# Transformer block, the pass for the row maxima: four 64x64 tiles instead of full-array matmuls, in eight groups among the first twelve score steps

## What is computed

```
content_score = einsum('bthd,bshd->bhts', q + u_bias, k)
pos_score = einsum('bthd,phd->bhtp', q + v_bias, p)
pos_score = _rel_shift(pos_score)
score = (content_score + pos_score) / math.sqrt(dh)
attn = jax.nn.softmax(score, axis=-1)
ctx = jnp.einsum('bhts,bshd->bthd', attn, v)
```

## Time and profile before

| | us |
|---|---|
| three runs | 1070.51, 1071.98, 1072.19 (median 1071.98) |
| profiled execution, its own time | 1072.0 |
| its span, first to last instruction | 1070.1 |
| busy in the span: PE, PEld | 850.5, 644.0 |
| busy in the span: DVE, ACT, POOL | 723.9, 460.0, 397.1 |
| mean granted clock of TensorE | 0.908 |

### The profile page before, as it was taken

The page is one execution under the profiler, slowest core; times in us unless marked ns, Lnnn a source line. Parts: engine busy times, 40 slices in busy tenths (PEclk is TensorE's granted clock), DMA queues, the critical chain, the costliest instruction groups (busy, mean ns, idle before and its releaser), DMA issues.

```text
span 1070.1 us, 21831 instructions
## 1 busy us (share of the span) xinstructions
PE 850.5 (79%) x8587; PEld 644.0 (60%) x8587; DVE 723.9 (68%) x1573; ACT 460.0 (43%) x773; POOL 397.1 (37%) x446
## 2 busy tenths in 40 slices
PE   2483679999999999987457998999999697057774
PEld 1243468888888888875434655666666377025553
DVE  6772435565555655533577888878788588989994
ACT  3860023333333333334455555656556554222331
POOL 6463001433334334335333334434243207323544
PEclk7696789999999999999669999999999899578998
DMA  6056111333243333453100000000000000000111
GB/s 140 1 159 216 42 39 38 79 75 65 67 94 72 72 65 69 90 153 74 25 1 1 2 2 2 2 2 2 1 2 1 1 1 1 0 0 2 23 26 32
DMA packets 69743, 46.45 MB, mean 43 GB/s; under 512 B 35184, under 2 KB 60984, under 8 KB 68920
## 3 DMA queue, kind: packets, MB, share of 16 engines
q1 hardware_dynamic: 52776, 24.72, 10.2%
q0 software_dynamic: 8032, 19.11, 7.0%
q10 hardware_dynamic: 8832, 1.22, 0.7%
HBM read 30.05 MB, written 12.06 MB: 39 GB/s over the span
## 4 chain that ended last, share of the span: by engine, by line
PE 40%; DVE 27%; DMA 9%; POOL 6%; SPq 6%; ACT 6%; issue 5%; ACTq 0%; POOLq 0%; DVEq 0%
PE PS L1059 7%; PE PS L1174 5%; PE PS L1175 5%; PE PS L1176 5%; PE PS L1079 4%; PE PS L1039 3%; PE PS L1063 3%; PE PS L1040 3%; DMA REG<-inverse_sums 3%; SPq L349 2%; DVE HB L1797 2%; DVE XX L1457 2%; DVE REG L1592 2%; DVE XX L1463 2%; DVE AM L1448 2%
## 5 line engine op out<-in xcount | busy, mean ns | idle before, releaser
L1573 DVE TENSOR_REDUCE MX<-PS 128x2 f32<-128x512 f32 x256 | 171.5, 686 | 165.4 <-PE PS L1040 163.7
L776 ACT ACTIVATE REG<-PS 128x1024 f32<-128x1024 f32 x128 | 131.5, 1027 | 242.1 <-PE PS L1063 239.4
L1059 PE MATMUL PS<-XX,TB 96*128 96x64 f16 x2048 | 160.2, 246 | 7.7 <-DMA XX<-NEG 4.5
L1039 PE MATMUL PS<-TM,YY 128*128 128x256 f16 x512 | 129.6, 285 | 31.7 <-DMA YY<-REG 14.9
L1059 PEld LDWEIGHTS PS<-XX,TB 96*128 96x128 f16 x2048 | 133.6, 120 | 23.2 <-issue 12.8
L613 POOL TENSOR_TENSOR HH<-HB,HH 128x512 f16<-128x512 f32 x64 | 75.8, 1184 | 173.8 <-ACT HH L833 173.8
L1040 PE MATMUL PS<-KM,YY 128*128 128x256 f16 x512 | 126.7, 279 | 0.0
L863 ACT ACTIVATE SG<-PS 128x512 f32<-128x512 f32 x128 | 76.2, 595 | 112.1 <-PE PS L1176 111.8
L1797 DVE SCALAR_TENSOR_TENSOR HB<-PS,SG 128x512 f32<-128x512 f32 x128 | 87.6, 684 | 46.0 <-ACT SG L863 46.0
L1063 PE MATMUL PS<-XX,KC 97*128 97x128 f16 x1024 | 108.0, 229 | 0.0
L1174 PE MATMUL PS<-XH,XX 128*128 128x512 f16 x256 | 98.8, 386 | 10.3 <-DVE HB L1797 10.1
(11 more groups left out here) (235 smaller groups left out, 1653.1 us busy)
## 6 DMA issues: line engine op xcount, KB each, us to landing
REG<-inverse_sums POOLq DMA_DIRECT2D x60, 128.0 KB, 3.1
YY<-queries_content ACTq DMA_DIRECT2D x224, 4.0 KB
KC<-keys_strips SPq DMA_DIRECT2D x16, 192.0 KB
keys_strips<-REG POOLq DMA_DIRECT2D x12, 224.0 KB, 7.8
R<-in_L_attn_x SPq DMA_DIRECT2D x32, 64.0 KB, 2.9
queries_position<-REG POOLq DMA_DIRECT2D x2, 960.0 KB, 12.9
queries_content<-REG POOLq DMA_DIRECT2D x2, 960.0 KB, 16.9
XX<-queries_position SPq DMA_DIRECT2D x60, 32.0 KB
```

Of the source, the lines that this page charges most:

```text
L776: A(P[jt][:, 1024 * up:1024 * up + 1024].rearrange("p (k x) -> p k x", k=2), ST[u % 2], ACT.Exp).then_inc(exp_done, 1)
L1039: mm(o, yp[:, a], TM[p][:, 31 - a:31 - a + T], start=True, stop=False)
L1059: mm(o_pos[:, a], TB[p][0:96, y0:y0 + 128], xp[0:96, 8 * bank + a], start=(a == 0), stop=False, skip_group_check=True)
L1573: nc.vector.tensor_reduce(MX[h % 2][:, 2 * kk:2 * kk + 2], banks[4 + kk % 2].rearrange("p (a j) -> p a j", a=2), AX_X, ALU.max)\
```

## The change

The maxima's matmuls become tiles of 64 rows and 64 columns. YP and YC hold half as many columns, with one half of the batches on partitions 0 to 63 and the other on 64 to 127, and TM's window is there twice. A group g (eight a head) does two offsets i times four tiles: first four position matmuls, then four content matmuls, 256 columns each, into two banks. One reduction takes 128x1024 to 128x4. Head 0's groups use banks 4, 5 and 6, 7 in turn; all later ones use banks 4 and 5 alone and wait for the reduction of the group just before. The groups follow score steps 0, 2, 3, 5, 7, 8, 10, 11, the context parts move to k = 3 and k = 11, and the second half of the shift is waited for at k = 4. Position queries always come from NQB, half by SyncE, half by GpSimd (by ScalarE for head 0); the copy in memory is gone. `shift_row` is four transfers, and XC's columns are laid out so that its content loads are contiguous.

```diff
+BANKS = (0, 4, 2, 6, 1, 5, 3, 7)
 NAT_K, NAT_QV, NAT_QU = 0, 2, 4
+BURSTS = (0, 2, 3, 5, 7, 8, 10, 11)
 
 
...
-    qvb_d = nc.dram_tensor("queries_position_batched", [128, N], F16, kind="Internal").ap()
...
-        YP, YC = ([YY[:, (2 * i + j) * N:(2 * i + j + 1) * N] for j in range(2)] for i in range(2))
+        YP, YC = ([YY[:, (2 * i + j) * N // 2:(2 * i + j + 1) * N // 2] for j in range(2)] for i in range(2))
...
-        Y_LOADS = 16 * (8 + 16 + 2)
...
+        def batch_pair(chunk):
+            b = 8 * (chunk % 2) + chunk // 2
+            return slice(b, b + 5, 4)
+        def maximum_queries(eng, h, src, half, done):
+            for s in range(8):
+                rows = 64 * half + 8 * (7 - s)
+                eng.dma_start(YP[h % 2][rows:rows + 8, :].rearrange("p (n s a) -> p s n a", n=8, s=8)[:, s],
+                              src[:, N // 2 * half:N // 2 * half + N // 2].rearrange("p (n s a) -> p s n a", n=8, s=8)[:, s])\
+                    .then_inc(done[h % 2], 16)
+        def maximum_banks(h, g):
+            return 6 if h == 0 and g % 2 else 4
 
...
-                sp.dma_start(TM[p][0:64, 0:287], window).then_inc(y_in[p], 16)
+                for half in range(2):
+                    sp.dma_start(TM[p][64 * half:64 * half + 64, 0:287], window).then_inc(y_in[p], 16)
 
...
-                                     NAT[NAT_QU + part][rows, :].rearrange("p (c w i) -> p w c i", c=4, w=4)[:, w]).then_inc(x_in[p], 16)
+                        sp.dma_start(XC[p][to:to + 8, 1024 * w:1024 * w + 1024],
+                                     NAT[NAT_QU + part][rows, 1024 * w:1024 * w + 1024]).then_inc(x_in[p], 16)
...
-            gp.dma_start(qvb_d[rest, :], NQB[rest, :]).then_inc(qvb_out, 16)
+            maximum_queries(gp, 1, NQB[DH:2 * DH, :], 1, y_second)
...
+            def later_queries(h):
+                if h < H:
+                    gp.wait_ge(max_mm, 8 * (h - 1))
+                    maximum_queries(gp, h, NQB[DH * h:DH * h + DH, :], 1, y_second)
             def sums_to_dram(h):
 
                 gp.wait_ge(ev_done, h + 1)
                 gp.dma_start(den_d[h % 2].rearrange("(g x) -> g x", g=4), EV[h % 2][DH:128:32, :]).then_inc(den_out, 16)
                 gp.wait_ge(den_out, 16 * (h + 1))
                 gp.dma_start(RC[h % 2][:, :], den_d[h % 2].rearrange("(p x) -> p x", p=128)).then_inc(den_in, 16)
+                later_queries(h + 3)
...
+            later_queries(2)
...
 
                 act.wait_ge(neg_ready, 2 * n + half + 1)
-                row = XC[n % 2][96:97, :].rearrange("p (m t a) -> p t m a", t=2, a=16)
-                act.dma_start(row[:, half], NEG[half][:, :]).then_inc(neg_in[half], 16)
+                row = XC[n % 2][96:97, :].rearrange("p (r m c t a) -> p r c t m a", r=2, m=64, c=2, t=2)
+                for r in range(2):
+                    for c in range(2):
+                        act.dma_start(row[:, r, c, half], NEG[half][64 * c:64 * c + 64, 8 * r:8 * r + 8]).then_inc(neg_in[half], 16)
 
             def content_rows(h, src, batches):
 
...
             act.wait_ge(high_done, 24)
-            for h in range(2):
-                content_rows(h, NAT[NAT_QU][DH * h:DH * h + DH, :], range(B))
+            content_rows(0, NAT[NAT_QU][0:DH, :], range(B))
+            maximum_queries(act, 0, NQB[0:DH, :], 1, y_in)
+            content_rows(1, NAT[NAT_QU][DH:2 * DH, :], range(10))
             shift_row(0, 0)
+            content_rows(1, NAT[NAT_QU][DH:2 * DH, :], range(10, B))
...
-            def maximum_scores(h, kk):
-                p, n = h % 2, 16 * h + kk
-                if kk == 0:
-                    pe.wait_ge(y_in[p], Y_LOADS * (h // 2 + 1))
-                if n >= 2:
-                    pe.wait_ge(max_done, n - 1)
+            def maximum_scores(h, g):
+                p, n, bank = h % 2, 8 * h + g, maximum_banks(h, g)
+                if g == 0:
+                    pe.wait_ge(y_in[p], Y_FIRST[p] + Y_LOADS * (h // 2))
+                    if h:
+                        pe.wait_ge(y_second[p], Y_SECOND * ((h + 1) // 2))
+                if h:
+                    pe.wait_ge(max_done, n)
+                elif g >= 2:
+                    pe.wait_ge(max_done, g - 1)
                 yp = YP[p][:, :].rearrange("p (m a) -> p a m", a=32)
                 yc = YC[p][:, :].rearrange("p (m a) -> p a m", a=32)
-                for half in range(2):
-                    a = 2 * kk + half
-                    o = banks[4 + kk % 2][:, T * half:T * half + T]
-                    mm(o, yp[:, a], TM[p][:, 31 - a:31 - a + T], start=True, stop=False)
-                    last = mm(o, yc[:, a], KM[p][:, :], start=False, stop=True)
+                for i in range(2):
+                    tiles = [(slice(64 * r, 64 * r + 64), 16 * c + 2 * g + i, banks[bank + r][64 * c:64 * c + 64, T * i:T * i + T])
+                             for r in range(2) for c in range(2)]
+                    for rows, a, o in tiles:
+                        mm(o, yp[rows, a], TM[p][rows, 31 - a:31 - a + T], start=True, stop=False)
+                    for rows, a, o in tiles:
+                        last = mm(o, yc[rows, a], KM[p][rows, :], start=False, stop=True)
                 last.then_inc(max_mm, 1)
...
-                    pe.wait_ge(neg_in[0], 16 * (h + 1))
-                elif k == 2:
-                    pe.wait_ge(neg_in[1], 16 * (h + 1))
+                    pe.wait_ge(neg_in[0], 64 * (h + 1))
+                elif k == 4:
+                    pe.wait_ge(neg_in[1], 64 * (h + 1))
...
@@ -1081,25 +1111,24 @@
                 if half:
                     last.then_inc(pv_mm, 1)
 
-            for kk in range(16):
-                maximum_scores(0, kk)
+            for g in range(8):
+                maximum_scores(0, g)
             for h in range(H):
                 for k in range(16):
                     scores(h, k)
-                    if h + 1 < H and k < 12:
-                        for kk in range(16 * k // 12, 16 * (k + 1) // 12):
-                            maximum_scores(h + 1, kk)
-                    if h and k == 4:
+                    if h + 1 < H and k in BURSTS:
+                        maximum_scores(h + 1, BURSTS.index(k))
+                    if h and k == 3:
                         context_part(h - 1, 1, 0)
                         context_part(h - 1, 1, 1)
-                    if k == 12:
+                    if k == 11:
                         context_part(h, 0, 0)
                         context_part(h, 0, 1)
             context_part(H - 1, 1, 0)
             context_part(H - 1, 1, 1)
...
-            def maximum(h, kk):
-                ve.wait_ge(max_mm, 16 * h + kk + 1)
-                nc.vector.tensor_reduce(MX[h % 2][:, 2 * kk:2 * kk + 2],
-                                        banks[4 + kk % 2].rearrange("p (a j) -> p a j", a=2), AX_X, ALU.max)\
+            def maximum(h, g):
+                bank = maximum_banks(h, g)
+                ve.wait_ge(max_mm, 8 * h + g + 1)
+                nc.vector.tensor_reduce(MX[h % 2][:, :].rearrange("p (r a) -> p r a", r=2)[:, :, 2 * g:2 * g + 2],
+                                        PS[:, bank:bank + 2, :].rearrange("p r (i j) -> p r i j", i=2), AX_X, ALU.max)\
                     .then_inc(max_done, 1)
 
             def negate(h, half):
 
-                ve.wait_ge(max_done, 16 * h + 8 * half + 8)
+                ve.wait_ge(max_done, 8 * h + 4 * half + 4)
                 if h:
-                    ve.wait_ge(neg_in[half], 16 * h)
...
+                   MX[h % 2][:, :].rearrange("p (r a) -> p r a", r=2)[:, :, 8 * half:8 * half + 8],
+                   -1.0, None, ALU.mult).then_inc(neg_ready, 1)
 
             def evacuate_context(h):
...
+            for g in range(8):
+                maximum(0, g)
+                if g % 4 == 3:
+                    negate(0, g // 4)
...
+                    for g in range(8):
+                        maximum(h + 1, g)
+                        if g % 4 == 3:
+                            negate(h + 1, g // 4)
+                        if g == 2 and h:
                             evacuate_context(h - 1)
-                        if kk == 14 and h:
+                        if g == 6 and h:
                             inverse_sums(h - 1)
```

More of the change, by code:

```diff
@@ L250, in adaln_program @@
         stored = sem("stored")
+        y_second = [sem(f"y_second{p}") for p in range(2)]
         l_feat, stored_last = sem("l_feat"), sem("stored_last")
@@ L344, in maximum_keys @@
                     .then_inc(y_in[h % 2], 16)
-            def maximum_queries(h, src):
-                for s in range(8):
-                    sp.dma_start(YP[h % 2][8 * (7 - s):8 * (7 - s) + 8, :].rearrange("p (b s a) -> p s b a", b=B, s=8)[:, s],
-                                 src.rearrange("p (b s a) -> p s b a", b=B, s=8)[:, s]).then_inc(y_in[h % 2], 16)
             def first_position_queries(h):
@@ L1117, in _ @@
                 for j in range(4):
```

(19 more changed lines are left out.)

59 lines of the change are left out of this document (29 added, 30 removed).

## The result

| | before | after |
|---|---|---|
| median of 15 runs each, us | 1073.74 | 1084.38 |
| lowest and highest | 1069.55, 1077.78 | 1077.70, 1090.81 |
| ratio of the means, after to before, with 95% interval | | 1.0106 [1.0081, 1.0130] |

The change makes the kernel about 11 us slower, where 1063 and a range up to 1078 were predicted. The profiled execution took 1086.14 us (its span 1084.3). The runs also scatter more than before.

The account below looks back on a forecast made before the run. It took the order of PE's own instructions to bound the heads. Steady heads -4.2, GpSimd +2, before head 1 -3.6, head 2's maxima +1.4 and last head -4.5 sum to -8.9: 1072.0 to 1063 us, range 1051 to 1078.

Parts of the forecast that it names:

- sum of a steady head: Heads 1 to 14: matmuls, new waits and dropped costs together change a head by -0.30 us, -4.2 in all.
- Before head 1: Start of the kernel: without the 896 KB copy SyncE's queue ends sooner, -3.6 us, between -6 and +2.
- last head: Wait for the shift shrinks by about 2 us and most low-clock time goes: -4.5, between 0 and -7.5.
- The exposed load of the first weights: Each maxima group: uncovered loading of its first weights costs 0.05 us, between nothing and 0.11.
- The new wait: Steady heads: a group waits 0.62 us for the previous reduction after one score step, three times a head; none after two.
- ScalarE's six more issues: Steady heads: six more shift transfers at about 0.4 us each cost nothing, at most 0.5 a head.
- GpSimd, +2: Heads: eight new query issues lengthen GpSimd's round by 2.3 us, making early heads' queries late; +2 us in all.
- The sign that was to give GpSimd away: Profile after: a steady period of 22.3 us or more, with no idle before GpSimd's first instruction, speaks for GpSimd.
- Head 2's maxima, +1.4: Head 2's maxima: ScalarE's content rows come behind three more shift transfers, 1.1 us, and 0.3 of head 0's new waits.
- GpSimd as bound: Rival: GpSimd's round, 21.4 to 24.2 us, bounds all heads; total about 1070 us; chance 0.15.
- tiles in turn: Rival: tiles do not run side by side, a round takes 0.22 us instead of 0.11; total 1113 us; chance 0.08.
- dearer switches: Rival: switching the array's shape costs 0.2 us each way, +0.9 a head; total 1076 us; chance 0.09.

Follow-up runs that it names:

- e1: Changed kernel with groups behind steps 1, 3, 4, 6, 8, 10, 11, 13, and the shift's second half behind a head's last exponential: 1077.85 us.
- e5: e1 with four of GpSimd's eight query transfers, for heads 2 on, moved to SyncE: 1058.08 us, ratio 0.9859 to the kernel before.
- e2: Changed kernel with the shift's second half issued in two pairs, behind the exponentials of steps 12 and 13 and of 14 and 15: 1084.09 us.
- e11: Changed kernel in its own order of groups, with four of GpSimd's eight query transfers of heads 2 on given to SyncE: 1087.70 us.
- e9: Changed kernel with head 2's content rows issued behind the first four exponentials of head 0 instead of the last two: 1072.58 us.
- e8: Kernel before the change, with the experts' weights issued only when the last shift has landed: 1069.70 us, ratio 0.9961.
- e12: Kernel before the change, with the experts' weights after the last shift and head 2's content rows behind head 0's first four exponentials: 1059.93 us.
- e6: e5 with the experts' weights issued only when the last shift has landed: 1051.83 us, ratio 0.9816 to the kernel before.
- e3: Changed kernel with the experts' weights issued by SyncE only when the last shift has landed: 1083.79 us, ratio 1.0103 to the kernel before.
- e10: e6 with head 2's content rows issued early as in e9: 1046.64 us, ratio 0.9745 to the kernel before.

## Why the prediction was wrong, by its steps

In short: the step that failed most is the sum of a steady head, where the exposed weight load (0.05 a group) and ScalarE's issues (nothing) were priced too low; the runs show 0.10 and 0.3. The steps on the start ("Before head 1") and on the last head failed next. The form of the steady head, tiles in parallel with three waits, was right.

- **Tiles side by side:** right. **Switches:** in 0.09 and out 0.09 to 0.10, right.
- **"The exposed load of the first weights I put at 0.05 us":** it is 0.10, near the upper bound of 0.11 that was named. A group is 0.75 us (entry 0.09, first round 0.21, two of 0.11, 0.01, exit 0.21, by the start times in the trace), eight are 6.0 instead of 5.52: +0.5 a head. The page TensorE: Matmul & The Clock Gate of the Trainium skill, section LDWEIGHTS (loading the stationary operand), puts a load at columns / 1.2 GHz. An estimate by that page is 53 ns for 64 columns; the trace shows 0.10 behind a switch, with four loads together.
- **The new wait, 0.62 three times a head, none at two steps:** right, 0.63. It was priced rightly and still not seen for what it was: at 1.9 us a head the largest cost of the change, and one of the order alone, as the heads of 20.5 us in e1 and e5 show.
- **ScalarE's six more issues, "nothing, and at most 0.5 a head":** 0.3 a head, shown by e2. The error was the duration: 0.60 each for four in a row, 2.42 us, against the 0.4 assumed (1.6 us), and a pair of steps is 1.34.
- **Sum of a steady head, -0.30:** with the measured terms -0.30 + 0.50 + 0.02 + 0.29 = +0.51; measured +0.42. Over 14 heads that is +5.9 instead of -4.2: 10.1 of the 21.4 us between the predicted 1063 and the measured 1084.4, **half of the whole error** and the step that failed most. The 0.09 between the two sums stays open.
- **GpSimd, +2:** 0 here (e11), since PE itself had become about as slow as GpSimd's round. That rounds would be 21.4 to 24.2 was right: without idle they are 22.9 in e1 and 23.0 in e9 on the mean, hardly more than PE's 22.72. The sign that was to give GpSimd away misleads here: the period is over 22.3, and in six of heads 1 to 13 its first instruction has no idle before it, yet taking four of its issues away changes nothing.
- **"Before head 1 ... -3.6":** +1.4, or nothing. The 896 KB are gone and the eight query transfers do take less (16.21 us instead of 19.30), but SyncE's issues ahead of them took more (the keys' strips ended at 78.7 instead of 76.4, KM took 7.34 instead of 4.96), so the queue was through at 102.4 instead of 100.8. Removing one large write did not shorten the queue that the path hangs on. Why these two grew was not tried. By the other profiles even the +1.4 is not clear: head 1's maxima start at 128.3, 129.0 and 130.5 us in the three of the kernel before (before, e8, e12) and at 127.8 to 130.2 in the seven with the changed kernel's order. So what is shown is that the gain did not come. Head 0's maxima started 6.5 us later and not 4; of this 1.5 reached its scores.
- **Head 2's maxima, +1.4:** +4.8 with what is carried over from head 1. The exponential ahead of the rows starts 2.6 later (150.90 against 148.28), and the shift transfers between it and the rows take 2.41 instead of 0.48: 1.9, again the price of the issue. e9 and e12 show that the wait itself comes from a place in ScalarE's order and that most of it was there before the change. The start of head 2's scores, 5.4 us later here, is no later than before in the spaced order (e1, e5, e6).
- **The last head, -4.5:** +0.6. The shift was expected 1.4 us later and came 3.6 later from the head's start (9.6 us in instead of 6.0). PE came to the wait 4.3 later, 3.2 by the later need (k = 4) and 0.9 by an exponential behind the four issues. So the wait shrank from 4.49 (the prediction has 4.7) to 3.88 only and not to 2.6, and the low clock that was to go stayed: five position blocks at about 1.05 us instead of three and a context. e3, e6 and e8 show that the weights' loads are the cause of the wait in both kernels.

Rivals: GpSimd as bound was not the cause here but is what e1 met; tiles in turn is excluded (rounds 0.11 apart); dearer switches are excluded too (0.09 to 0.10), what was dearer was the load behind them.

## What to carry to other kernels

When a change packs more small pieces, count each switch with the whole uncovered weight load behind it, and give each issue the price that several in a row have on their queue, not that of one. A single-buffered result is cheap if the order puts enough other work between its users: here the same pass in another order, with the query transfers shared out, is 1.4% faster than before instead of 1.1% slower (e5). The 2.5% of e10 are not all the tiles': the two edits that have nothing to do with them give the kernel before 1.3% (e12). Before crediting a change with a wait that it shortens, see whether a move of one issue removes the wait in both kernels, and compare with that.

## What was unexpected of the hardware

An engine off the path cost time by where its transfers fell: the same four shift transfers, issued at the same 0.23 to 2.1 us of a head, had landed by 5.3 us when four transfers of 128 KB on another queue had been issued from 2.8 us ahead of the head on (e1, head 2), and only at 8.2 when these were issued from 0.8 us into it (e1, head 5); PE started k = 4 at 6.06 and 8.22. One wait of 9.3 us for a transfer cost 12 us: in the 6 us from 160 on the granted clock was 0.50, in the next 6 it was 0.55. And from head 1's first maxima to its scores the same instructions took 28.9 us in one execution (e3) and 21.5 in another (e11), with a granted clock of 0.56 and 0.90 and no wait for a transfer in either.
